# Summing the weight magnitudes inside the head loop and making the ternary weights beside the last attention head

## The reference

```python
x = x + xattn(layernorm(x), ctx)     # 16 heads; rotary tables on q (384 wide) and on the context
h = layernorm(x)
gate = silu(bit_linear(h, gate_w, gate_b)); val = bit_linear(h, val_w, val_b)   # 512 -> 2048
x = x + bit_linear(gate * val, out_w, out_b)                                     # 2048 -> 512

def bit_linear(x, w, b):
    gamma_x = clip(max(abs(x), axis=-1), 1e-5, None)          # one per token
    x_dq = clip(round(x * 127 / gamma_x), -128, 127) * gamma_x / 127
    gamma_w = clip(mean(abs(w)), 1e-5, None)                  # one per weight matrix
    w_dq = clip(round(w / gamma_w), -1, 1) * gamma_w
    return einsum(x_dq, w_dq) + b
```

## Time and profile before

| | |
|---|---|
| median of 3 runs | 983.46 us (982.33 to 986.01) |
| the profiled execution | 983.45 us, its span 981.7 us |
| PE busy | 869.4 us (89%) |
| DVE busy | 845.0 us (86%) |
| ACT busy | 530.4 us (54%) |
| POOL busy | 511.0 us (52%) |
| DMA | 39.14 MB, 40 GB/s over the span |

### The profile page before, as it was taken

The page is one execution under the profiler, slowest core; times in us unless marked ns, Lnnn a source line. Parts: engine busy times, 40 slices in busy tenths (PEclk is TensorE's granted clock), DMA queues, the critical chain, the costliest instruction groups (busy, mean ns, idle before and its releaser), DMA issues. The chain is left out here.

```text
span 981.7 us, 15230 instructions
## 1 busy us (share of the span) xinstructions
PE 869.4 (89%) x4294; PEld 667.5 (68%) x4294; DVE 845.0 (86%) x1232; ACT 530.4 (54%) x865; POOL 511.0 (52%) x527
## 2 busy tenths in 40 slices
PE   3657999999999999999999999999999776049996
PEld 2435778888888888888888887888888554024442
DVE  6666989989998998899889989998998555979994
ACT  2235556555655656466555555655655587774331
POOL 5284664657465746564655557465746103615541
PEclk9778999999999999999999999999999898559998
DMA  7000100000000000100000010000000640400000
GB/s 276 1 24 15 29 15 24 25 17 24 13 24 18 24 13 26 29 19 18 25 16 24 13 28 24 13 24 17 24 13 24 266 176 1 181 1 12 21 21 33
DMA packets 21718, 39.14 MB, mean 40 GB/s; under 512 B 5056, under 2 KB 11456, under 8 KB 20416
## 3 DMA queue, kind: packets, MB, share of 16 engines
q1 hardware_dynamic: 20608, 36.77, 11.3%
q10 hardware_dynamic: 1088, 2.10, 0.6%
HBM read 36.77 MB, written 2.10 MB: 40 GB/s over the span
## 5 line engine op out<-in xcount | busy, mean ns | idle before, releaser
L647 POOL TENSOR_TENSOR rot_cos<-rot_cos,rot_sin 128x512 f32<-128x512 f32 x93 | 120.3, 1293 | 139.9 <-DVE rot_sin L844 128.4
L732 ACT CAST pt_hi<-banks 128x512 fp32r<-128x512 f32 x256 | 138.4, 595 | 85.5 <-PE banks L1010 85.5
L748 ACT ACTIVATE probs<-scores,neg_max 128x1024 f32<-128x1024 f32 x128 | 143.9, 1125 | 71.6 <-DVE neg_max L868 70.9
L835 DVE TENSOR_TENSOR pt_lo<-banks,pt_hi 128x512 fp32r<-128x512 f32 x256 | 164.5, 683 | 16.7 <-ACT pt_hi L732 14.4
L868 DVE TENSOR_REDUCE neg_max<-scores 128x1 f32<-128x1024 f32 x128 | 155.8, 1218 | 9.8 <-PE scores L1027 8.8
L1010 PE MATMUL banks<-ident,probs 128*128 128x128 f32 x1024 | 135.0, 275 | 8.1 <-ACT probs L748 6.5
L1010 PEld LDWEIGHTS banks<-ident,probs 128*128 128x128 f32 x1024 | 120.5, 142 | 27.2 <-DVE acc L863 5.5
L655 POOL TENSOR_TENSOR rot_lo<-rot_cos,rot_hi 128x512 fp32r<-128x512 f32 x93 | 119.8, 1288 | 7.8
L945 PE MATMUL banks<-pt_hi,v_hi 128*128 128x512 f32 x256 | 103.3, 404 | 2.9 <-DVE pt_lo L835 1.9
L863 DVE SCALAR_TENSOR_TENSOR acc<-banks,inv,acc 128x512 f32<-128x512 f32 x128 | 92.6, 746 | 13.3 <-PE banks L945 11.4
L945 PE MATMUL banks<-pt_hi,v_lo 128*128 128x512 f32 x256 | 101.2, 395 | 0.0
(11 more groups left out here) (184 smaller groups left out, 1966.9 us busy)
## 6 DMA issues: line engine op xcount, KB each, us to landing
load<-in_pack SPq DMA_DIRECT2D x15, 320.0 KB, 2.9
load<-in_pack SPq DMA_DIRECT2D x16, 256.0 KB, 2.7
raw_early<-in_gate_w SPq DMA_DIRECT2D x4, 1024.0 KB, 8.3
raw_early<-in_val_w SPq DMA_DIRECT2D x4, 1024.0 KB, 16.1
load<-in_pack SPq DMA_DIRECT2D x16, 192.0 KB, 2.4
acc<-in_x ACTq DMA_DIRECT2D x4, 512.0 KB, 7.2
load<-in_pack SPq DMA_DIRECT2D x16, 128.0 KB, 2.1
raw_early<-in_out_w SPq DMA_DIRECT2D x2, 1024.0 KB, 22.3
```

What stands on the lines that cost most here:

```text
L647: nc.gpsimd.tensor_tensor(total, total, rot_sin[:, c, :], ALU.add).then_inc(rot_sum, 1)
L732: nc.scalar.copy(out, src).then_inc(group_hi, 1)
L748: nc.scalar.activation(probs[:, u % 2, :], scores[:, u % 2, :], ACT.Exp, bias=neg_max[:, u:u + 1], accum_out=sums[:, u:u + 1]).then_inc(ex ...
L835: return nc.vector.tensor_tensor(pair[1], src, pair[0].bitcast(F32), ALU.subtract)
```

## The change

1. **Magnitudes in the loop.** The three matrices are summed as 24 chunks of 128 x 1024 (512 KB), three in two heads: SP loads a chunk into one buffer `raw_chunk` (`load_chunk`), and ACT sums it (`("abs", w)` in `ACT_ORDER`), behind exponential 2 in every period and behind exponential 5 in odd ones; one chunk is summed in the preparation, ahead of the high part of the values, and two in the first period. The weights are so loaded twice. `rot_lo` is now written over `rot_cos`, and the group `C` of batch 1 stands ahead of `B` in the first period.
2. **The last head** gets its own lists `LAST_PE`, `LAST_ACT`, `LAST_DVE`, in place of `last` and `FINISH`. All three weight scales come at its start (`G`). SP loads the raw lots into three slots, each again once its lot is dropped to bf16. POOL lifts and clips ten lots (`lift_and_clip`), ACT drops them (`("drop", n)`). Behind batch 0's output DVE takes its statistics, `spread` and `scales`; ACT norms its four token tiles, POOL lifts them, PE turns them (`X`) and DVE writes `xt`.
3. **`ffn_weights` is gone.** In feed-forward tile 0 POOL makes lots 10 and 11 and DVE takes batch 1's statistics; in tile 1 come its scales, and its four token tiles are normed, lifted, turned and taken between the tile's own work. The output bias is added tile by tile on POOL.
4. **The last feed-forward tile** is worked in pieces: the range in four parts, lift, rounding, turning, copy and output product in two halves.
5. `V` waits for each half of its transposes where its matmuls need it.

```diff
+LAST_ACT = (
+    ("double", 1, "last"), ("T", 7, 0, "last"), ("T", 7, 1, "last"), ("exp", 0), ("exp", 1), ("drop", 0), V1,
+    ("T", 0, 0), ("T", 0, 1), ("T", 1, 0), ("exp", 2), ("drop", 1), ("T", 1, 1), ("exp", 3), ("T", 2, 0), ("T", 2, 1),
+    ("exp", 4), ("T", 3, 0), ("T", 3, 1), ("exp", 5), ("drop", 2), ("drop", 3), ("drop", 4), ("M",), V0, ("T", 4, 0),
+    ("T", 4, 1), ("T", 5, 0), ("exp", 6), ("drop", 5), ("T", 5, 1), ("exp", 7), ("T", 6, 0), ("T", 6, 1), ("T", 7, 0),
+    ("drop", 6), ("T", 7, 1), ("drop", 7), ("drop", 8), ("V", 1), ("root", 0), ("drop", 9), ("norm", 0), ("norm", 1),
+    ("norm", 2), ("norm", 3),
+)
...
+LAST_DVE = (
...
+    ("O", 1, 3, "last"), ("max", 7), ("M",), V0, ("T", 4, 0), ("T", 4, 1), ("T", 5, 0), ("O", 0, 0), ("O", 0, 1),
+    ("O", 0, 2), ("O", 0, 3), ("T", 5, 1), ("stats", 2), ("T", 6, 0), ("T", 6, 1), ("T", 7, 0), ("stats", 3),
+    ("T", 7, 1), ("stats", 0), ("stats", 1), ("spread", 0), ("V", 1), ("scale", 0), ("O", 1, 0), ("O", 1, 1),
+    ("O", 1, 2), ("O", 1, 3), ("X", 0), ("X", 1), ("X", 2), ("X", 3),
+)
...
-        starts = [n for n, item in enumerate(PE_ORDER) if item == A1 or item[:2] == ("part", 0) and item[3] == A1]
-        behind = PE_ORDER[starts[0]:] if orders is PE_ORDER else order_of(PE_ORDER[starts[0]:])
+        starts = PE_ORDER.index(("B", 0, 0, "next"))
+        behind = PE_ORDER[starts:] if orders is PE_ORDER else order_of(PE_ORDER[starts:])
...
+    def statistics(self, dve, u):
+        nc, tile, one = self.nc, self.t["acc"][:, u, :], slice(u, u + 1)
+        nc.vector.bn_stats(self.stats[:, u, :], tile)
+        nc.vector.tensor_reduce(self.most[:, one], tile, AX, ALU.max)
+        nc.vector.tensor_reduce(self.least[:, one], tile, AX, ALU.min).then_inc(self.seen, 1)
...
+    def spread(self, dve, b):
+        nc, half = self.nc, slice(b * U, (b + 1) * U)
+        link = lambda ins: self.link(dve, ins)
+        mean, var = self.mv[:, half, 0], self.mv[:, half, 1]
+        var_eps, most, least = (x[:, half] for x in (self.var_eps, self.most, self.least))
+        dve.wait_ge(self.seen, U * (b + 1))
+        for u in range(b * U, (b + 1) * U):
+            ins = nc.vector.bn_aggr(self.mv[:, u, :], self.stats[:, u, :])
+        link(ins)
+        nc.vector.tensor_scalar(var_eps, var, EPS, None, ALU.add).then_inc(self.var_ready, 1)
+        nc.vector.tensor_tensor(most, most, mean, ALU.subtract)
+        link(nc.vector.tensor_tensor(least, mean, least, ALU.subtract))
+        link(nc.vector.tensor_tensor(most, most, least, ALU.max))
...
+    def scales(self, dve, b):
+        nc, t, half = self.nc, self.t, slice(b * U, (b + 1) * U)
+        link = lambda ins: self.link(dve, ins)
+        mean, factor, x_gamma, tmp = self.mv[:, half, 0], self.factor[:, half], t["x_gamma"][:, half], self.tmp[:, half]
+        rstd = self.rstd[:, half]
+        inverse_deviation(nc, dve, self.var_eps[:, half], self.root[:, half], rstd, tmp, self.root_ready, b + 1, link)
+        link(nc.vector.tensor_tensor(tmp, self.most[:, half], rstd, ALU.mult))
+        link(nc.vector.tensor_scalar(x_gamma, tmp, 1e-5, 1.0 / 127.0, ALU.max, ALU.mult))
+        link(nc.vector.reciprocal(self.x_scale[:, half], x_gamma))
+        link(nc.vector.tensor_tensor(factor, rstd, self.x_scale[:, half], ALU.mult))
+        nc.vector.scalar_tensor_tensor(out=self.shift[:, half], in0=mean, scalar=-1.0, in1=factor, op0=ALU.mult,
+                                       op1=ALU.mult).then_inc(self.scale_ready, 1)
+        for w, name in enumerate(("x_gate", "x_val")):
+            nc.vector.tensor_scalar(t[name][:, half], x_gamma, t["gamma"][:, w:w + 1], None, ALU.mult)
...
+    def normalize(self, act, u):
+        act.wait_ge(self.scale_ready, u // U + 1)
+        if u >= 2:
+            act.wait_ge(self.lifted_ready, u - 1)
+        self.nc.scalar.activation(self.normed[:, u % 2, :], self.t["acc"][:, u, :], ACT.Identity, bias=self.shift[:, u:u + 1],
+                                  scale=self.factor[:, u:u + 1]).then_inc(self.normed_ready, 1)
+    def lift(self, pool, u):
+        pool.wait_ge(self.normed_ready, u + 1)
+        self.nc.gpsimd.tensor_scalar(self.lifted[:, u % 2, :], self.normed[:, u % 2, :], MAGIC, MAGIC + 127, ALU.add,
+                                     ALU.min).then_inc(self.lifted_ready, 1)
...
+            def load_chunk(h, w):
+                n = chunk_number(h, w)
+                if h.i is not None or n:
+                    sp.wait_ge(summed, n)
+                if h.i is None:
+                    src = chunk_rows[w][0:P, :]
+                else:
+                    sp.nop(nofuse=True)
+                    src = chunk_rows[w][bass.ds(h.i * P + P, P), :]
+                sp.dma_start(raw_chunk[:], src).then_inc(chunk_loaded, 16)
...
+            def add_up(h, w):
+                n = chunk_number(h, w)
+                act.wait_ge(chunk_loaded, n * 16 + 16)
+                if h.i is not None:
+                    act.nop(nofuse=True)
+                column = t["partial"][:, w:w + 1] if h.i is None else t["partial"][:, bass.ds(n, 1)]
+                nc.scalar.activation(raw_chunk[:], raw_chunk[:], ACT.Abs, accum_out=column).then_inc(summed, 1)
...
+                if kind == "V":
+                    places += [p.place(("T", U * group[1] + U - 1, c // 4) + mark) for c in chunks if c % 4 == 0]
...
+    def load(self, sp, n):
+        if n >= RAW_SLOTS:
+            sp.wait_ge(self.dropped, n - RAW_SLOTS + 1)
+        src = raw_lot(self.sources, n)
+        sp.dma_start(self.lot(n).rearrange("p (c n) -> p c n", c=src.shape[1]), src).then_inc(self.loaded[n % RAW_SLOTS], 16)
+    def lift_and_clip(self, pool, n):
+        lot, w = self.lot(n), n // RAW_PARTS
+        pool.wait_ge(self.loaded[n % RAW_SLOTS], 16 * (n // RAW_SLOTS + 1))
+        self.nc.gpsimd.tensor_scalar(lot, lot, self.t["inv_gamma"][:, w:w + 1], MAGIC, ALU.mult, ALU.add).then_inc(self.lifted, 1)
+        pool.wait_ge(self.lifted, n + 1)
+        self.nc.gpsimd.tensor_scalar(lot, lot, MAGIC + 1, MAGIC - 1, ALU.min, ALU.max).then_inc(self.clipped, 1)
+    def drop(self, act, n):
+        act.wait_ge(self.clipped, n + 1)
+        self.nc.scalar.activation(self.place(n), self.lot(n), ACT.Identity, bias=self.t["minus_magic"][:]).then_inc(self.dropped, 1)
...
+                    if before == 1 and n % 2 and n > 1:
+                        turn_tokens(U + n // 2 - 1)
+                    if before == 1 and n == NP - 1:
+                        turn_tokens(NU - 1)
...
+                    if before == 0 and n % 2:
+                        second.statistics(dve, U + n // 2)
+                    if before == 0 and n == NP - 1:
+                        second.spread(dve, 1)
+                    if before == 1 and n == 1:
+                        second.scales(dve, 1)
+                    if before == 1 and n in (4, 6):
+                        take(U + n // 2 - 2)
+                    if before == 1 and n == NP - 1:
+                        take(NU - 2)
+                        take(NU - 1)
...
-                range_of(h7)
+                last_range(h7)
+                last_round(h7, 0)
                 finish(h6)
-                round_down(h7)
-                copy_ht(h7)
+                last_copy(h7, 0)
+                last_round(h7, 1)
+                last_copy(h7, 1)
                 finish(h7)
...
+                    if before == 1:
+                        second.normalize(act, U + n)
+                    if before == 0 and n == 1 or before == 1 and n == NH - 1:
+                        raw.drop(act, LOTS_WITH_HEAD + before)
+                if before == 0:
+                    second.deviation_root(act, 1)
...
+                if before == 0:
+                    raw.lift_and_clip(pool, LOTS_WITH_HEAD)
+                    pool.wait_ge(out_bias_loaded, 16)
+                if h.number >= U or before == 2:
+                    pool.wait_ge(second.normed_ready, NU)
+                add_bias(h)
```

More of the change, by code:

```diff
@@ L64 @@
 A0, A1, V1, V0, C0, C1 = ("A", 0, "next"), ("A", 1, "next"), ("V", 1, "last"), ("V", 0), ("C", 0, "next"), ("C", 1, "next")
-UNGROUPED = ("score", "max", "exp", "sum", "double")
+UNGROUPED = ("score", "max", "exp", "sum", "double", "abs", "drop", "stats", "spread", "root", "scale", "norm")
 PE_ORDER = (
@@ L129, in done_by, with schedule_of @@
     return item
-def schedule_of(orders, odd, first=False, last=False):
+def schedule_of(orders, odd, first=False):
     def kept(item):
@@ L147, in schedule_of @@
             schedule.insert(min(schedule.index(item) for item in behind if item in schedule), ("double", 1))
-    if last and orders is not ACT_ORDER:
-        at = schedule.index(("O", 0, 0))
-        schedule[at:at] = [("sum", 0), ("G", 0)]
     return schedule
@@ L764, in prepare @@
                 high_part(p, ("A", 1))
+                add_up(p.head, 2)
                 start.values_high(act, 0)
@@ L998, in products @@
                     b = group[1]
```

(20 more changed lines are left out.)

525 lines of the change are left out of this document (242 added, 283 removed).

## The result

The change takes the kernel from 984.19 us (982.33 to 986.01, 4 runs) to 968.94 us (966.75 to 969.66, 4 runs): a ratio of 0.984 (95% interval 0.9815 to 0.9867), about 15 us. The profiled execution has a span of 967.6 us where the one before has 981.7. The forecast said 958.0 (947 to 971): the direction and most of the size are right, 11 us of the forecast gain are missing. The 968.94 us lie outside the 951 to 965 to which the forecast gave its largest chance, and inside the 947 to 971.

A forecast was written before the change was run, and what follows sets the result against it. PE bounds the loop and feed-forward tiles 2 to 7; it idles between, while DVE and ACT round lots and norm tokens. 0 + 1 - 43.8 + 21 - 3.5 = -25.3 us, giving 958 us (947 to 971).

The forecast's parts named there:

- The loop, 0: Head loop: ACT's sums of magnitudes fit its idle time and PE stays full, so 0 us, at most 8.
- The start, +1: Preparation and first period: one sum delays the values' high part and the batch 1 group moves; +1 us, 0 to +3.
- The block, -43.8: Last head's start to first feed-forward product: 63 us against 106.8, so -43.8, bounds -52.8 to -34.8.
- The conveyor: Last head: raw lots pass through three slots, loaded by SP, clipped by POOL at 4.07 us each, dropped by ACT.
- V of batch 1 ends on PE at +47, and its high part stands behind drop 8, at +49.5: Last head, us behind its start: ACT's drop of lot 8 ends at +49.5 and holds V's high part until then.
- the +55.5 of the forecast: Last head: DVE's small links after V's high part end 55.5 us behind the stage's start, then the token norms follow.
- Feed-forward, +21: Feed-forward tiles 0 and 1: tile 2's first gate at +40.4 against +19.4 before, so +21 us, bounds +11.5 to +25.
- The others follow at 2 to 3 us each: Feed-forward tile 1: after token 5 at about +32, the remaining tokens pass the five-engine chain at 2 to 3 us each.
- PE's list, which the forecast named: Feed-forward tile 1: token transposes stand in PE's list between its products, so the products behind them wait.
- The tail, -3.5: Last feed-forward tile in parts: range 1.4 sooner, lift's first half 1, overlap about 1; -3.5 us, bounds -1 to -6.5.
- the lower bound: Last feed-forward tile: -6.5 us if the output product also runs at full clock.
- the conveyor's time (967 to 970): Rival, last head: lots arrive 2 us later each round, V's high part at +58, block 72 us; chance 0.18.

The follow-up runs named there:

- the second profile: The changed kernel itself run once more, unaltered, for another profile: 970.43 us, ratio 0.9859.
- The quick form alone: The changed kernel with POOL's token lift as multiply by 1 and add the magic number, without the clamp at 127: 960.96 us.
- experiment 9: Two kernels: the change with the last tile in one piece, 972.26 us; the kernel before with the last tile in halves, 981.10 us against 983.38.

## Why the prediction was nearly right

- **The loop, 0:** right, in its size and its reason. PE is full, and without the sums the periods are no shorter.
- **The start, +1:** 3.0 in the profile, at the upper bound. 1.06 of it is the sum ahead of the high part of the values, as said. The rest is not shown to be the change's: the same code differs by that much between executions.
- **The block, -43.8:** -42.2 (-41.2 in the second profile). The number is right, and two errors in its working nearly cancel, which is luck. The conveyor ran as forecast: lots 4 to 9 were clipped at +27.1, +34.8, +38.8, +42.9, +46.9 and +51.2, where I had +27.5, +35.5, +39.5, +43.5, +47.5 and +52.5. The step "V of batch 1 ends on PE at +47, and its high part stands behind drop 8, at +49.5" failed: PE ended V at +49.6, because half of V ran at a granted clock of 0.50 behind two waits, and the high part waited for PE. Drop 8 ended at +48.9, so the two were 0.7 us apart. Behind it the links of `scales` ran unblocked, and the first norm still came at +53.8, 1.7 before the +55.5 of the forecast. Then the token stage took 10.8 us where I had 6 and a gap of 1.5; 4.3 of that were the slow form of the lift.
- **Feed-forward, +21:** the step that failed, +28.3. Tile 0 ended at +19.0 (forecast +19.5), with the links blocked as said, and the norms started at +23.3. What was mis-sized is the token chain: "The others follow at 2 to 3 us each" became 6.7, 4.1 and 4.2 us between transposes, because each lift took 1.92 (one, beside DVE's work, 2.90). The quick form alone takes 6.1 us off; PE's list, which the forecast named, is worth 4 more. Of the 7.3 us of error, 5.0 lie before tile 2's first gate (+45.4 against +40.4). The other 2.3 lie between that gate and the first output product, 4.8 us against 2.6 before, and the forecast put nothing there: PE now starts tile 2's products only behind the last copy of a token, at 879.85. With the quick lift the gate comes at +38.6, sooner than forecast, and these 2 to 3 us stay.
- **The tail, -3.5:** -3.1 in the profiles; by the runs of halves against whole -2.3, and -1.8 to -3.3. The number is right and the reason is not. The 3.5 were to be overlap, with the product beginning 2 to 3 us sooner; it began 1.0 sooner in the two profiles, and 1.4 and 1.8 in the pairs of experiment 9. The other 2.0 us are the product's own time, 6.6 and 4.6 us at granted clocks of 0.54 and 0.78. The forecast gave the product the 0.83 of the whole stage, and had its time in the lower bound but not in the sum.
- **Sum:** +2.0, +1.6, +7.3 and +0.4 are the errors of the four stretches, 11.3 us. Of the rivals, the conveyor's time (967 to 970) came out, but not its mechanism: lots did not come late and V's high part did not come at +58. Only its remark that PE, when it waits, is granted the lower clock is seen, in V (0.50).

## What to carry to other kernels

Price every new instruction by a row of the same engine and the same operations, not by its shape. The lift had no price here, and the row that matches it in engine and shape alone (0.62 for 128x512) would have been off by three. When engine work is moved beside a stage, halve it in an experiment before calling it the bound; POOL with 39 of 52 us busy was not. Read the clock over the stretch of the instructions that you price, and not over their stage: the last product ran at 0.54 in a stage of 0.83. And when transposes sit in a matrix engine's in-order list, their producers' delay is paid by the products behind them; it pays to shorten the producer first, then to move the transposes.
